# A state-space mixer's result norm: its root taken in the next loop's merged chain, scan rows cut at the diagonal, and a causal copy moved ahead of the step factors

## The reference

```python
def mixer(x, ...):
    zgate, u, Bc, Cc, dt = split(x @ in_proj_w.T)
    u, Bc, Cc = silu(causal_conv(u, Bc, Cc) + conv_b)
    Bc, Cc = Bc * rsqrt(sum(Bc * Bc) + 1e-6), Cc * rsqrt(sum(Cc * Cc) + 1e-6)
    dt = softplus(dt + dt_bias)
    # per token: z = (z + dt * (u B - A y)) / (1 + dt * dt * A);  y = y + dt * z;  out = y . C
    return (scan_out + D_skip * u) * silu(zgate) @ out_proj_w.T + out_proj_b

def block_forward(x, ...):
    x = x + mixer(rms(x, norm1_w), ...)
    h = gelu(rms(x, norm2_w) @ fc1_w.T + fc1_b)
    return x + h @ fc2_w.T + fc2_b
```

## Time and profile before

| | |
|---|---|
| median of three executions | 2106.72 us |
| profiled execution, its own time | 2104.22 us |
| span of the profiled execution (first to last instruction) | 2102.4 us |
| mean granted TensorE clock | 0.962 of full speed |
| busy: PE, PE weight loads, DVE, ACT, POOL | 1902.8, 1148.1, 1325.0, 986.6, 415.4 us |
| POOL works in the mixer alone | 415.39 us of its 415.4 before 850 us |

### The profile page before, as it was taken

The page is one execution under the profiler, slowest core; times in us unless marked ns, Lnnn a source line. Parts: engine busy times, 40 slices in busy tenths (PEclk is TensorE's granted clock), DMA queues, the critical chain, the costliest instruction groups (busy, mean ns, idle before and its releaser), DMA issues.

```text
span 2102.4 us, 28315 instructions
## 1 busy us (share of the span) xinstructions
PE 1902.8 (91%) x9472; PEld 1148.1 (55%) x9472; DVE 1325.0 (63%) x4021; ACT 986.6 (47%) x2374; POOL 415.4 (20%) x569
## 2 busy tenths in 40 slices
PE   4569899899898679899999999999999999999986
PEld 2447666676676445445545545545555555555553
DVE  5668888878875356537737636646745755755632
ACT  3453553553541145635634644644644544554631
POOL 4675675675572010000000000000000000000000
PEclk8789999999999879999999999999999999999998
DMA  3000000000000261111111111112111111111100
GB/s 117 1 0 10 18 1 18 18 1 19 9 1 9 69 180 45 56 37 50 52 46 50 53 45 50 51 40 57 48 43 53 49 46 50 52 46 41 38 20 9
DMA packets 63520, 84.19 MB, mean 40 GB/s; under 512 B 5104, under 2 KB 61984, under 8 KB 62480
## 3 DMA queue, kind: packets, MB, share of 16 engines
q1 hardware_dynamic: 62912, 81.92, 13.7%
q10 hardware_dynamic: 464, 0.46, 0.1%
HBM read 75.02 MB, written 7.34 MB: 39 GB/s over the span
## 4 chain that ended last, share of the span: by engine, by line
PE 57%; DVE 4%; ACT 3%; issue 1%; DMA 0%; DVEq 0%; ACTq 0%
PE x_ps L1260 18%; PE x_ps L1253 10%; PE x_ps L1215 8%; PE x_ps L1238 8%; PE x_ps L1222 8%; ACT x_pT L1387 2%; PE x_ps L1329 2%; PE x_ps L1314 1%; DVE x_bn L981 1%; PE x_ps L1322 1%; PE x_ps L1267 1%; DVE x_pr L1502 1%; PE x_ps L1335 1%; DVE x_pr L1493 1%; ACT x_pr L1393 0%
## 5 line engine op out<-in xcount | busy, mean ns | idle before, releaser
L1493 DVE CUSTOM_DVE_ANT_0 x_pr<-x_ps,x_mk 128x375 f32<-128x375 f32 x448 | 227.9, 546 | 398.5 <-issue 302.4
L1387 ACT ACTIVATE x_pT<-x_ps 125x384 f32<-125x384 f32 x448 | 196.0, 489 | 419.5 <-PE x_ps L1222 418.8
L1393 ACT ACTIVATE x_pr<-x_pr,x_mx 128x375 f32<-128x375 f32 x448 | 268.1, 607 | 46.4 <-DVE x_mx L1493 45.9
L1222 PEld LDWEIGHTS x_ps<-ident,x_pr 128*125 128x125 f32 x1344 | 166.2, 190 | 127.3 <-issue 109.7
L1215 PE MATMUL x_ps<-x_kT,x_qT 64*128 64x375 f32 x896 | 206.5, 537 | 13.4 <-DVE x_mx L1493 8.3
L1222 PE MATMUL x_ps<-ident,x_pr 128*125 128x128 f32 x1344 | 209.5, 293 | 6.8 <-DVE x_pr L1502 6.8
L1260 PE MATMUL x_ps<-x_xn,x_w 128*128 128x448 f32 x512 | 213.6, 548 | 0.0
L1238 PE MATMUL x_ps<-x_pT,x_va 125*64 125x256 f32 (+1 forms) x1536 | 177.1, 366 | 27.5 <-ACT x_pT L1387 27.5
L1502 DVE TENSOR_SCALAR x_pr<-x_pr,x_rc 128x375 f32<-128x375 f32 x448 | 170.9, 424 | 8.0
L1238 PEld LDWEIGHTS x_ps<-x_pT,x_va 125*64 125x64 f32 x1536 | 95.8, 138 | 110.9 <-ACT x_pT L1387 42.2
L254 PE MATMUL m_ps<-m_xa,w_in 128*128 128x448 f32 x352 | 146.4, 563 | 10.2 <-ACT m_xa L451 10.2
(11 more groups left out here) (168 smaller groups left out, 2982.2 us busy)
## 6 DMA issues: line engine op xcount, KB each, us to landing
x_mk<-in_mask SPq DMA_DIRECT2D x224, 187.5 KB, 2.3
x_cx<-in_context SPq DMA_DIRECT2D x32, 375.0 KB
x_mixed<-m_x SPq DMA_DIRECT2D x8, 448.0 KB, 3.3
X<-x_mixed SPq DMA_DIRECT2D x8, 448.0 KB, 4.0
out<-f_so SPq DMA_DIRECT2D x8, 448.0 KB, 3.4
m_X<-in_x SPq DMA_DIRECT2D x7, 448.0 KB, 4.8
fc<-in_fc SPq DMA_DIRECT2D x2, 1024.0 KB, 12.5
x_w<-in_x_w SPq DMA_DIRECT2D x1, 2048.0 KB, 17.9
```

Source lines behind the costliest of these rows:

```text
L1222: last = pe.transpose(bank(2 + e)[0:JP, t * ROWS:(t + 1) * ROWS], pr[:, 2 * (p % SLOT) + e, t * JP:(t + 1) * JP], ident[:, :])
L1387: act.activation(pT[:, 4 * (batch(p) % 2) + 2 * (p % NP % 2) + e, :, :].rearrange("p t s -> p (t s)"), bank(2 + e)[0:JP, 0:JT * ROWS], ACT ...
L1393: act.activation(pr[:, k, :], pr[:, k, :], ACT.Exp, scale=-1.0, bias=mx[:, k:k + 1], accum_out=sums[:, k:k + 1]).then_inc(h_e.sem, 1)
L1493: dve.tensor_tensor_reduce(pr[:, k + e, :], bank(e)[:, 0:J], mk[:, p % SLOT, :], -1.0, 3.0e38, ALU.add, ALU.min, mx[:, k + e:k + e + 1]).t ...
```

## The change

It has these parts:
- `result_b` keeps the sums and the statistics. The root of result i-3 is taken by `roots(i)` in `tiles(i)`: `v` and `rr` have 20 columns for 16. The new `normed_result(i-3)` applies it in `tiles(i)` between `scale_bc` and `left`, for i >= 3. Results 5, 6 and 7 get chains of their own behind the last loop's `scaled_b`, `result_b(6)` and `result_b(7)` (`roots_result`); the last second-norm root is `roots_last`.
- x1 has a ring of XR = 3 instead of 2, `x_out` too. `sq` has one buffer instead of two, so each square waits for the one before. SP issues `tokens_out(i-1)` where it issued `tokens_out(i)`.
- The scan's matmuls take `(j+1)*Q` rows of `Rb` for block j (16 to 112) instead of 112. VectorE sets the first four PSUM banks to zero once, and PE waits for that before its first transposes.
- `factors(i+1)` stands in `scan(i)` between causal part 0 and causal part 1; it stood behind `softplus(i+1)` at the end of the loop before.

```diff
-        sq = sb("m_sq", [S, 2, D])
+        sq = sb("m_sq", [S, D])
-        rr = sb("m_rr", [S, 16])
+        rr = sb("m_rr", [S, 20])
-        x1 = sb("m_x1", [S, 2, GB, D])
+        x1 = sb("m_x1", [S, XR, GB, D])
...
+                if i >= 1:
+                    tokens_out(i - 1)
+            tokens_out(NG - 1)
...
                         for j in blocks:
                             for c in range(2):
-                                last = pe.matmul(bank(2 * (b % 2) + half)[0:S, (j % 4) * 128:(j % 4 + 1) * 128],
-                                                 Rb[:, c, b, j * S:(j + 1) * S], Lm[:, c, b * NQ + j, :, :],
+                                rows = (j + 1) * Q
+                                last = pe.matmul(bank(2 * (b % 2) + half)[0:rows, (j % 4) * 128:(j % 4 + 1) * 128],
+                                                 Rb[:, c, b, j * S:j * S + rows], Lm[:, c, b * NQ + j, :, :],
                                                  start=(c == 0), stop=(c == 1))
...
             pe.wait_ge(i_in, 16)
+            pe.wait_ge(s_psum.sem, 1)
             turn_tokens(0)
...
-                    if b >= 2:
-                        hold(act, done, i, b - 1)
-                    act.activation(sq[:, b % 2, :], src(b), ACT.Square, accum_out=dst[:, b:b + 1]).then_inc(done.sem, 1)
+                    if b >= 1:
+                        hold(act, done, i, b)
+                    act.activation(sq[:, :], src(b), ACT.Square, accum_out=dst[:, b:b + 1]).then_inc(done.sem, 1)
...
+            def roots(i):
+
+                sums, v, y, t = st[:, 0:8], st[:, 8:28], rr[:, :], st[:, 28:48]
...
+                hold(dve, b_ln, i - 3, 2 * GB)
+                dve.tensor_scalar(v[:, 16:20], mv[:, :, 1], LN_EPS, None, ALU.add).then_inc(a_rr.sem, 1)
...
+                rsqrt(dve, v, y, t, a_rr, i, 3)
+
+            def roots_last():
+                v, y, t = st[:, 8:12], rr[:, GB:2 * GB], st[:, 28:32]
...
+            def roots_result(i, k):
+                v, y, t = st[:, 8:12], rr[:, 16:20], st[:, 28:32]
+                dve.wait_ge(b_ln.sem, b_ln.value(i, 2 * GB))
+                dve.tensor_scalar(v, mv[:, :, 1], LN_EPS, None, ALU.add).then_inc(b_lr.sem, 1)
+                dve.wait_ge(b_lr.sem, b_lr.value(k, 1))
+                rsqrt(dve, v, y, t, b_lr, k, 1)
...
                 causal_part(i, 0)
+                between()
                 for b in range(1, GB):
                     causal_part(i, b)
                     gate(b - 1)
                 gate(GB - 1)
...
-                norm_root(dve, i, mv, st[:, 40:52], b_ln, GB)
-                norm_apply(dve, lambda b: x1[:, i % 2, b, :], lambda b: x1[:, i % 2, b, :], mv, st[:, 40:52], b_ln, GB)
+                norm_stats(dve, i, lambda b: x1[:, i % XR, b, :], bn, mv, b_ln, GB, ready=ready)
+
+            def normed_result(i):
+                for b in range(GB):
+                    dst = x1[:, i % XR, b, :]
+                    dve.tensor_scalar(dst, dst, mv[:, b, 0:1], rr[:, 16 + b:17 + b], ALU.subtract, ALU.mult).then_inc(b_out.sem, 1)
...
                 gate_part(i, 3)
                 scale_bc(i)
+                if i >= 3:
+                    normed_result(i - 3)
                 left(i)
                 u_parts(i)
 
             dve.memset(MTs[:, :, :, :, :], 0.0).then_inc(s_zero.sem, 1)
+            dve.memset(PS[:, 0:4, :], 0.0).then_inc(s_psum.sem, 1)
             dve.memset(st[:, 4:8], 1.0).then_inc(s_one.sem, 1)
+            dve.memset(mv[:, :, :], 1.0).then_inc(s_one.sem, 1)
...
             for i in range(NG):
-                scan(i)
+                scan(i, (lambda: factors(i + 1)) if i + 1 < NG else (lambda: None))
                 if i + 1 < NG:
                     tiles(i + 1)
                 else:
                     mixed_b(i)
-                    roots(NG, bc=False)
+                    roots_last()
                     scaled_b(i)
+                    roots_result(NG - 3, 1)
+                    normed_result(NG - 3)
                 if i >= 1:
                     result_b(i - 1)
                 if i + 2 < NG:
                     softplus(i + 2)
-                    factors(i + 2)
+            roots_result(NG - 2, 2)
+            normed_result(NG - 2)
             result_b(NG - 1)
+            roots_result(NG - 1, 3)
+            normed_result(NG - 1)
```

More of the change, by code:

```diff
@@ L155, in mixer @@
         s_one = count("m_one", 0)
+        s_psum = count("m_psum", 0)
         x_in = [count(f"m_xin{n}", 16) for n in range(XR)]
-        x_out = [count(f"m_xout{n}", 16) for n in range(2)]
+        x_out = [count(f"m_xout{n}", 16) for n in range(XR)]
         a_sq = count("a_sq", GB)
@@ L171, in mixer @@
         a_bst = count("a_bst", 1)
-        a_rr = count("a_rr", 2 + RSQRT)
+        a_rr = count("a_rr", 3 + RSQRT)
         a_bb = count("a_bb", 2)
@@ L198, in mixer @@
         b_s = count("b_s", 2)
-        b_ln = count("b_ln", LN)
+        b_ln = count("b_ln", 2 * GB)
+        b_lr = count("b_lr", 1 + RSQRT)
+        b_out = count("b_out", GB)
         block = ctx.enter_context(nc.Block())
@@ L218, in tokens_out @@
             def tokens_out(i):
-                sp.wait_ge(b_ln.sem, b_ln.value(i, LN))
-                sp.dma_start(xm_dram[i * GB:(i + 1) * GB, :, :].rearrange("b s d -> s b d"), x1[:, i % 2, :, :]).then_inc(x_out[i % 2].sem, 16)
+                sp.wait_ge(b_out.sem, b_out.value(i, GB))
+                sp.dma_start(xm_dram[i * GB:(i + 1) * GB, :, :].rearrange("b s d -> s b d"), x1[:, i % XR, :, :]).then_inc(x_out[i % XR].sem, 16)
             dt_bc = 3 * 128
@@ L235, in _ @@
                     tokens_in(i + XR)
-                tokens_out(i)
-            for c in range(2):
-                sp.wait_ge(x_out[c].sem, x_out[c].value(NG // 2, 0))
+                if i >= 1:
+                    tokens_out(i - 1)
+            tokens_out(NG - 1)
+            for i in range(NG - XR, NG):
+                sp.wait_ge(x_out[i % XR].sem, x_out[i % XR].value(i // XR + 1, 0))
         @block.tensor
@@ L455, in squares_b @@
                 hold(act, a_sq, min(i + 2, NG - 1), GB)
-                square_sums(i, lambda b: x1[:, i % 2, b, :], b_sq, st[:, 4:8])
+                square_sums(i, lambda b: x1[:, i % XR, b, :], b_sq, st[:, 4:8])
             def step_parts(i):
@@ L574, in _ @@
         def _(dve):
-            def roots(i, bc=True):
-                sums, v, y, t = st[:, 0:8], st[:, 8:24], rr[:, :], st[:, 24:40]
-                if bc:
-                    dve.wait_ge(a_bst.sem, a_bst.value(i, 1))
-                    dve.tensor_scalar(v[:, 8:16], bank(5)[0:S, 0:8], 4.0 * BC_EPS, None, ALU.add).then_inc(a_rr.sem, 1)
+            def roots(i):
+                sums, v, y, t = st[:, 0:8], st[:, 8:28], rr[:, :], st[:, 28:48]
+                dve.wait_ge(a_bst.sem, a_bst.value(i, 1))
+                dve.tensor_scalar(v[:, 8:16], bank(5)[0:S, 0:8], 4.0 * BC_EPS, None, ALU.add).then_inc(a_rr.sem, 1)
@@ L581, in roots @@
                 hold(dve, b_sq, i - 1, GB)
                 hold(dve, a_sq, min(i + 1, NG - 1), GB)
-                dve.tensor_scalar(v[:, 0:8], sums, 1.0 / D, RMS_EPS, ALU.mult, ALU.add).then_inc(a_rr.sem, 1 if bc else 2)
-                hold(dve, a_nv, min(i, NG - 1), GB)
+                dve.tensor_scalar(v[:, 0:8], sums, 1.0 / D, RMS_EPS, ALU.mult, ALU.add).then_inc(a_rr.sem, 1)
+                hold(dve, b_ln, i - 3, 2 * GB)
+                dve.tensor_scalar(v[:, 16:20], mv[:, :, 1], LN_EPS, None, ALU.add).then_inc(a_rr.sem, 1)
@@ L585, in roots @@
+                hold(dve, a_nv, i, GB)
                 hold(dve, a_bb, i - 1, 2)
-                dve.wait_ge(a_rr.sem, a_rr.value(i, 2))
-                rsqrt(dve, v, y, t, a_rr, i, 2)
+                dve.wait_ge(a_rr.sem, a_rr.value(i, 3))
+                rsqrt(dve, v, y, t, a_rr, i, 3)
+            def roots_last():
+                v, y, t = st[:, 8:12], rr[:, GB:2 * GB], st[:, 28:32]
+                dve.wait_ge(b_sq.sem, b_sq.value(NG - 1, GB))
+                dve.tensor_scalar(v, st[:, 4:8], 1.0 / D, RMS_EPS, ALU.mult, ALU.add).then_inc(b_lr.sem, 1)
+                dve.wait_ge(b_lr.sem, 1)
+                rsqrt(dve, v, y, t, b_lr, 0, 1)
@@ L688, in causal_part, with scan @@
                                         bank(2 * (b % 2) + half)[0:S, 0:(j1 - j0) * 128]).then_inc(b_mc.sem, 1)
-            def scan(i):
+            def scan(i, between):
                 def gate(b):
@@ L721, in ready @@
                         dve.wait_ge(b_r.sem, b_r.value(i, 4))
-                        dst = x1[:, i % 2, 2 * c:2 * c + 2, :]
+                        dst = x1[:, i % XR, 2 * c:2 * c + 2, :]
                         dve.tensor_tensor(dst, bank(4 + c)[0:S, :].rearrange("p (b d) -> p b d", d=D), dst, ALU.add).then_inc(b_s.sem, 1)
                         dve.wait_ge(b_s.sem, b_s.value(i, c + 1))
-                norm_stats(dve, i, lambda b: x1[:, i % 2, b, :], bn, mv, b_ln, GB, ready=ready)
-                norm_root(dve, i, mv, st[:, 40:52], b_ln, GB)
```

(6 more changed lines are left out.)

12 lines of the change are left out of this document (6 added, 6 removed).

## The result

The changed kernel takes **2083.23 us** (median of four executions, 2079.94 to 2086.39) against 2106.43 of the kernel before (four, 2103.86 to 2109.41): ratio 0.9889, 95% interval 0.9869 to 0.991. That is 23.2 us, more than four times what I had forecast, and 9 us outside my range. The profiled execution took 2082.22 us with a span of 2080.4.

The account below looks back on a forecast made before the run. PE was taken to wait in the scan stretches for VectorE's late causal copy. Terms 12.9 + 3.5 - 1.2 - 10.0 - 0.4 = 4.8 us gained, so 2106.72 - 4.8 = 2101.9 us; likeliest 2098 to 2106, range 2092 to 2110.

Parts of the forecast that it names:

- stretches 1 to 6: Scan stretches of loops 1 to 6: merged root chain and factors behind copy 0 gain 12.9 us.
- loop 0: Scan stretch of loop 0: the copy no longer waits 5.64 us for factors; 3.5 us gained of 9.7 lost.
- width changes in loop 7: Loop 7's scan matmuls with cut rows: changes of output width lie bare on PE, 1.2 us lost.
- application in front of `left`: From tiles(3) on, four operations between dB and the two L676 delay `left` and ACT's copies: 10.0 us lost.
- single `sq`: One `sq` buffer makes each square wait for the reading before; bare only at the last turn, 0.4 us lost.
- The sign that I had named for being wrong: Wait before L307 at the end of `down`: under 1.5 us, against a forecast near 3, would mean 2093 us.
- my 0.85 us of cover: ACT's Lm copies after dB: ACT is busy until 293.85, so 0.85 of the 3.0 us delay is swallowed.
- 18.3 us a stretch: Each scan stretch of loops 1 to 6, including POOL blocking some gates' products; PE by itself would need 17.45.
- up to 2 us later: Softplus ends some 1 us before the scan starts, or this much later where POOL's residual sums stand in its way.
- The application is cheap: Rival, chance 0.22: POOL takes no turns with the application, so its 10.0 us loss shrinks to about 1.5: 2093 us.
- Free width changes: Rival, chance 0.13: the scan matmuls' width changes cost nothing, 4.7 us better: 2097 us.
- The slow rival: Rival, chance 0.20: the wait before L307 reaches 4.35 us and the clock falls, 6.4 us slower: 2113.1 us.

Follow-up runs that it names:

- the split one: Changed kernel with all 112 rows and the factors in two pieces, the two products E only after causal copy 3: 2078.14 us, ratio 0.986 to before.
- root-only run: Changed kernel with all 112 rows and the factors back behind softplus, leaving the merged root alone of VectorE's two order edits: 2091.94 us, ratio 0.9936 to before.

## Why the prediction was wrong

Its reading of what bounds the kernel holds, and so does the sign. The sum was 4.8 us; the terms as measured:

| term | forecast | measured |
|---|---|---|
| stretches 1 to 6 | +12.9 | 122.67 - 106.43 = +16.2 |
| loop 0 | +3.5 | 25.92 - 22.55 = +3.4 |
| width changes in loop 7 | -1.2 | 16.21 - 17.31 = -1.1 |
| application in front of `left` (sum of the waits before the transposes) | -10.0 | 4.41 - 4.15 = +0.3 |
| single `sq` | -0.4 | -0.15 (the last wait for `turn_mixed`, 7.03 for 6.88) |
| sum | +4.8 | +18.6 |

The start of attention moved by 19.1: these 18.6 and the 1.1 of the earlier loop 0, less some 0.1 us a loop that no term here covers. The +0.3 is a net: -1.7 for the application, by the run with it in the idle time, and +1.9 for two waits of 1.46 us that are gone.

**The step that failed** is "The result's application moves in front of `left`": 10.0 us were charged for it, and it cost 1.7. Two of its links were off and one was missing. The sign that I had named for being wrong, a wait before the transposes below 1.5 us, came true.
- "Four operations cost 4 x 0.3 and up to three of POOL's 0.6: 3.0 us." The four took 2.41 us, near enough. But I added them to the two L676 as they stood, 1.12 and 1.08 us, each of which already held half a microsecond of waiting for POOL. That waiting was paid once: by the time L698 came, only one of POOL's four products was left, and it let VectorE go first. `left` ended 3.39 us after dB instead of 2.22: 1.2 us later, not 3.0.
- Of that my 0.85 us of cover (ACT busy with its bias copy L526) took most. ACT's copies started 3.42 us after dB instead of 3.03: 0.39 goes on, not 2.2. The run with the application in the idle time confirms it, 0.50 us of wait for 0.92, and the run with eight more operations shows that nothing more is swallowed behind ACT, since there 4.59 us more at ACT became 4.63 us more at PE.
- What I had left out is the other end. ACT's row from the first copy to the last tanh is 12.53 us long in both kernels; the last silu behind it took 1.59 us where POOL blocked it and 0.62 where not. Before, that was so in every other loop, hence 1.46 and 0.5 us of wait; this is the silu of loop 3:

```profile
385.57 0.62 DVE L615 SCALAR_TENSOR_TENSOR m_u<-m_th,m_u 128x448 f32<-128x448 f32 x1 [1.01 <-ACT m_th L474]
```

After it the silu takes 0.62 in all of them. That comes from which operations of VectorE and POOL meet, but why they meet so stays open: the wait is 0.5 in every loop with the factors moved alone, and 1.46 again in one loop with the cut rows alone. 0.5 + 0.39 is the 0.92 us of the trace, in four loops; a fifth, for which I had counted 1.2, has no wait.

**A term mis-sized**: 18.3 us a stretch, measured 17.74, or 3.3 us over six. The steps inside it stand (copy 0 copied at 4.15, forecast 4.2; causal 1 done at 10.9, forecast 11.1), each a little shorter than I had it, and I had put 0.3 us on top for POOL's blocking of the gates. It was already at PE's own limit: I had 17.45 for PE, the trace has 17.53. One addition in my working was off: the four parts of copy 0 come to 4.35, not 4.2, and 4.35 is what the later times go on from.

**What held.** Copy 0 first and factors behind it; no wait of more than 0.2 us left; the clock back at 1.00; 1.1 us for the width changes in a bare loop, in part by luck (ten changes at 0.11 us, not some seven at 0.17); no gain from narrower weights. Softplus starts as soon as ACT's L471 is done, 8.84 us ahead of the scan (317.51 - 308.67; 404.44 - 395.66 = 8.78 in my working), but takes 10.3 us beside POOL's sums and ends 1.44 us into it, within the "up to 2 us later" that I had allowed. What I had not seen is how little the two moves add up: 11.5 and 16.7 us alone, 22.3 together.

**The rivals.** "The application is cheap" was the right one, for a reason other than mine: POOL does take turns with it. With its 1.5 us in place of 10.0 and the stretch as measured the sum is 4.8 + 8.5 + 3.3 = 16.6 us, near the 19.1. Free width changes are refuted by 17.31 against 16.21. The slow rival, the clock falling before the transposes, did not come, but it lay nearer than I said: I had it decide at 4.35 us of wait, but the clock fell behind a wait of 1.76 us in every other loop of the run with the application behind `left`, and behind 1.44 us in one loop of four in the split one, while before it stayed at 1.00 behind 3.19 us. What decides it from loop to loop stays open: the wait of 2.16 us in the root-only run left the stretch at 0.91 in loops 3 and 5 and at 1.00 in loops 2, 4 and 6.

## What to carry to other kernels

- A duration in a trace may hold a wait. Before adding work in front of two blocked operations, take their undisturbed time (0.61 us here) and lay out anew who meets whom; adding 3.0 us of blocked work to 2.2 of blocked work counted the same wait twice.
- Cut long VectorE work where a copy that TensorE waits for can go between: moving 5.7 us of factors behind one copy was worth 16.7 us, and cutting them once more the rest of the stretch. Put work without a deadline where its engine idles, even if it takes five times as long there (6.05 us for 1.13): it cost PE nothing.
- Fewer weight columns bought nothing here, with a moving side of 128 columns, and each crossing of 32 or 64 columns cost 0.11 us.
